# One block of 64-row products per batch in a gated cross-attention and mixture-of-experts kernel: score banks by half of the heads, weighed back into the same banks, and rows of maxima a batch sooner

## The reference, cut to what matters

```python
# per batch t of 32: x[t] is 128 tokens x 128, ctx[t] is 128 keys x 64; 16 heads of 64
x = x + tanh(g_xattn) * xattn(layernorm(x), ctx_512, Wq, Wk, Wv, Wo, bo)
x = x + tanh(g_ffn) * ffn(layernorm(x), ...)      # 32 experts, 8 taken per token, and a shared one

def xattn(q, kv, ...):
    scores = (q @ Wq)_h @ (kv @ Wk)_h.T * scale   # 16 heads, 128 x 128 each
    attn = softmax(scores)
    return concat_h(attn @ (kv @ Wv)_h) @ Wo + bo
```

## Time and profile before

| | |
|---|---|
| median of 3 runs | 651.04 us (650.0 to 651.46) |
| time of the profiled execution | 651.89 us |
| its span, first to last instruction | 650.0 us |
| instructions | 14071 |
| PE busy | 639.0 us (98%) |
| DVE busy | 532.0 us (82%) |
| ACT busy | 389.9 us (60%) |
| POOL busy | 329.3 us (51%) |
| granted clock | full in all 40 slices |

### The profile page before, as it was taken

One profiled execution on the slowest core, in us unless ns is written; L12 is line 12 of the kernel. 1 busy time (PEld: TensorE's weight loads), 2 busy tenths in 40 slices (PEclk: granted clock), 3 DMA queues, 4 the chain that ended last, 5 costly groups with the idle time before them and its releaser, 6 DMA issues.

```text
span 650.0 us, 14071 instructions
## 1 busy us (share of the span) xinstructions
PE 639.0 (98%) x3763; PEld 483.8 (74%) x3763; DVE 532.0 (82%) x1362; ACT 389.9 (60%) x739; POOL 329.3 (51%) x388
## 2 busy tenths in 40 slices
PE   8999999999999999999999999999999999999998
PEld 6657776777766777667558878787887878788786
DVE  6889989888898888988878969778695977869565
ACT  3665666667666676665565555555656555555554
POOL 4336544345534355343404656566575655657563
PEclk9999999999999999999999999999999999999999
DMA  6243343232332324323326555353746535364550
GB/s 181 67 108 80 68 96 85 63 85 60 96 85 60 85 60 96 86 60 82 83 60 172 136 134 131 82 134 85 163 114 134 136 78 132 87 161 114 134 146 17
DMA packets 58429, 65.60 MB, mean 101 GB/s; under 512 B 26256, under 2 KB 35344, under 8 KB 58384
## 3 DMA queue, kind: packets, MB, share of 16 engines
q1 hardware_dynamic: 58384, 65.07, 41.1%
HBM read 61.64 MB, written 2.88 MB: 99 GB/s over the span
## 4 chain that ended last, share of the span: by engine, by line
PE 94%; DVE 2%; ACT 2%; issue 1%; DMA 1%; SPq 0%; DVEq 0%
PE bank L1291 17%; PE bank L1292 17%; PE bank L1293 17%; PE bank L1391 10%; PE bank L1415 9%; PE bank L1338 4%; PE bank L1358 3%; PE bank L1367 2%; PE bank L1361 2%; PE bank L1364 2%; PE bank L1378 2%; DVE halves L880 2%; PE bank L1379 1%; PE bank L1381 1%; ACT halves L628 1%; PE bank L1298 1%
## 5 line engine op out<-in xcount | busy, mean ns | idle before, releaser
L602 POOL TENSOR_TENSOR halves<-area,halves 128x512 fp32r<-128x512 f32 x134 | 174.4, 1302 | 138.5 <-ACT halves L759 133.0
L780 ACT ACTIVATE area<-bank 128x512 f32<-128x512 f32 x136 | 81.4, 599 | 111.1 <-PE bank L1293 108.3
L1247 DVE TENSOR_TENSOR bank<-area,bank 128x512 f32<-128x512 f32 x128 | 88.6, 692 | 50.8 <-PE bank L1293 50.5
L697 ACT ACTIVATE area<-bank 128x512 f32<-128x512 f32 x128 | 69.5, 595 | 100.1 <-PE bank L1367 100.1
L1291 PE MATMUL bank<-x2t_hi,w_hi 128*128 128x512 f32 x272 | 110.3, 405 | 0.1
L1292 PE MATMUL bank<-x2t_hi,w_lo 128*128 128x512 f32 x272 | 107.2, 394 | 0.0
L1293 PE MATMUL bank<-x2t_lo,w_hi 128*128 128x512 f32 x272 | 106.3, 391 | 0.0
L759 ACT ACTIVATE halves<-area 128x512 fp32r<-128x512 f32 x136 | 85.1, 626 | 17.1 <-DVE area L1258 15.9
L889 DVE TENSOR_REDUCE row_max<-bank 128x4 f32<-128x512 f32 x128 | 82.2, 685 | 6.9 <-PE bank L1338 5.9
L1258 DVE TENSOR_TENSOR area<-bank,wbc 128x512 f32<-128x512 f32 x128 | 86.3, 679 | 0.0
L529 POOL TENSOR_TENSOR ctx_hi<-ctx_raw,ones_col 128x128 fp32r<-128x128 f32 x32 | 14.9, 464 | 139.1 <-DMA ctx_raw<-ctx_t 122.1
(11 more groups left out here) (164 smaller groups left out, 1259.4 us busy)
## 6 DMA issues: line engine op xcount, KB each, us to landing
wbc<-rows_dram SPq DMA_DIRECT2D x126, 256.0 KB, 4.5
inverse_bc<-inverse_dram SPq DMA_DIRECT2D x64, 256.0 KB, 3.8
...
ctx_raw<-ctx_t SPq DMA_DIRECT2D x32, 64.0 KB, 3.5
ctx_keys<-ctx_nat SPq DMA_DIRECT2D x32, 64.0 KB, 2.1
...
max_rows<-max_t SPq DMA_DIRECT2D x64, 4.0 KB
```

The costliest lines, as they stand in the source:

```text
L602: nc.gpsimd.tensor_tensor(hid_lo[:, u % SLOTS, :], hid[:, u % HIDS, :], raw(hid_hi[:, u % SLOTS, :]), ALU.subtract).then_inc(hidlo_ready, 1)
L697: nc.scalar.activation(probs_t[:, k, :, :], st_ps[q][:].rearrange("p (h n) -> p h n", h=4), ACT.Exp)\
L780: nc.scalar.activation(silu_g[:, u % 2, :], gate_ps[u % 2][:], ACT.Silu).then_inc(silu_ready, 1)
L1247: nc.vector.tensor_tensor(up_ps[u % UPS][:], silu_g[:, u % 2, :], up_ps[u % UPS][:], ALU.mult)\
```

## The change

The change moves no arithmetic and adds none. It changes four things.

1. The banks: half 0 of the heads has its scores in banks 2 and 3, half 1 in banks 4 and 5. The weighed sums of a half go back into the banks of its scores, once ACT has taken the exponentials. `g_project` borrows banks 0, 1, 6 and 2 inside the attention stage. `scores` of a half now waits until `u_out` of the same half of the batch before has emptied the banks.
2. The order on PE: `max_scores` of half 0, `scores` of both halves and `max_scores` of half 1 follow each other, and all full-row work of the batch stands behind them. `weigh` of half 1 belongs to its own batch and ends it.
3. The row maxima of batch t+2 are transposed, copied out and loaded in batch t, where those of batch t+1 were before.
4. The orders on ACT, DVE and SP follow, and the statistics of x in chunk 0 stand at other places.

```diff
-STATS_AT = {2: (2,), 3: (3, 4), 4: (5,), 5: (6,), 6: (7,)}
+STATS_AT = {1: (2, 3), 2: (4, 5), 3: (6, 7)}
...
-        scores_ps, st_ps, u_ps, ut_ps, small_ps = bank[0:2], bank[2:4], bank[4:6], bank[6], bank[7]
+        scores_ps, ut_ps, small_ps = bank[0:2], bank[6], bank[7]
+        st_ps = (bank[2:4], bank[4:6])
+        u_ps = st_ps
+        g_ps = (bank[0], bank[1], bank[6], bank[2])
...
@@ SP, attention
+                    if not (first and b == 0):
+                        spread_sums(t - 1, (b - 1) % CB)
                     if not last:
                         wait_first(ctx_ready, t + 1)
                         load_raw(b, (t + CB) * P)
-                    if not (last and b == CB - 1):
-                        load_max_row(t + 1, (b + 1) % 2, t - 1)
-                    if not (first and b == 0):
-                        spread_sums(t - 1, (b - 1) % CB)
...
                         store_inverse(t - 1, (b - 1) % 2)
+                    if not (last and b >= 2):
+                        load_max_row(t + 2, b % 2, t)
+                    if not (first and b == 0):
                         spread_inverse(t - 1, (b - 1) % 2)
...
@@ ACT, attention (after exp_of(t, 0, 0) and exp_of(t, 0, 1))
+                    if not first and not last:
+                        probs_high(t)
+                    exp_of(t, 1, 0)
+                    exp_of(t, 1, 1)
+                    if b == 1 and not last:
+                        xt_high(c + 1)
...
+                    for q in range(2):
+                        u_out(t, b, 0, q)
+                    if not (last and b >= 2):
+                        max_out(t + 2, b % 2, 2 * c + b // 2 + 1)
...
                     if b % 2 == 1 and not last:
                         g_high(2 * c + 2 + b // 2, b // 2)
...
+                    for q in range(2):
+                        u_out(t, b, 1, q)
...
@@ DVE, steady_attention
-                    for q in range(2):
-                        take_max(t + 2, b % 2, 0, q)
+                    take_maxima(t + 2, b % 2, 0)
                     batch_stats(t - CB, b)
                     if b == 0:
                         ln_apply(c + 1, t + CB)
+                    batch_mean(t - CB, b)
+                    take_maxima(t + 2, b % 2, 1)
                     probs_low(t)
                     if b == 1:
                         xt_low(c + 1)
-                    for q in range(2):
-                        take_max(t + 2, b % 2, 1, q)
                     residual(t - 3)
-                    batch_mean(t - CB, b)
                     if b == CB - 1:
                         keep_means(t - b - CB)
+                    if b % 2 == 0:
+                        invert(t - 1, (b - 1) % 2)
+                    normalise(t - 2, (b - 2) % CB, 0)
                     if b % 2 == 1:
                         g_low(2 * c + 2 + b // 2, b // 2)
                         invert(t - 1, (b - 1) % 2)
-                    normalise(t - 2, (b - 2) % CB, 0)
-                    if b % 2 == 0:
-                        invert(t - 1, (b - 1) % 2)
                     normalise(t - 2, (b - 2) % CB, 1)
...
@@ PE, scores
-                wait(pe, exp_ready, 4 * t + 2 * h)
+                wait(pe, u_ready, 4 * t + 2 * h - 2)
...
@@ PE, attention (all batches but the first)
+                        if not (last and b >= 2):
+                            max_scores(t + 2, b + 2, nth + 1, 0)
+                        scores(t, b, nth, 0, nth + 1, projections)
+                        scores(t, b, nth, 1, nth + 1, None)
+                        if not (last and b >= 2):
+                            max_scores(t + 2, b + 2, nth + 1, 1)
+                    if b == 1:
                         transpose_norm(c + 1, ut_ps)
...
                     if not (first and b < 3):
                         project_out(t - 3, (b + 1) % 2, t + 1 if last and b == CB - 1 else t + 2)
...
+                    for q in range(2):
+                        if first or last:
+                            weigh(t, b, 0, q, c + 1)
+                        else:
+                            weigh_halves(t, b, q)
+                    if not (last and b >= 2):
+                        transpose_max(t + 2, b % 2)
...
                     if b % 2 == 1 and not last:
-                        g_project(b // 2, c + 1, ((max_ready, 4 * (t + 2) + 3), (exp_ready, 4 * t + 3)))
...
+                        g_project(b // 2, c + 1, ((max_ready, 4 * (t + 2) + 3), (u_ready, 4 * t)), range(4), g_ps)
+                    for q in range(2):
+                        weigh(t, b, 1, q, c + 1)
```

233 lines of the change are left out of this document (94 added, 139 removed).

## The result

The changed kernel takes 662.38 us (median of 4 runs), the kernel before 651.19 beside it: ratio 1.0168, 95% interval 1.0144 to 1.0192. The forecast of 646.2 with a range to 651.3 was wrong, and on the wrong side. The profiled execution has a span of 660.5 us against 650.0, so 10.5 us have to be found.

The account below looks back on a forecast made before the run. PE was taken as the bound, busy 639.0 of 650.0 us, with DVE second to watch. Gains of 15.6 us less losses of 10.8 gave -4.8 from a median of 651.04, so 646.2 us, range 641.5 to 651.3.

Parts of the forecast that it names:

- On SP `load_max_row` now stands ahead of `spread_inverse` ... the inverses are wanted a batch later, so I cost it at nothing: SP's queue: the new order delays the inverses by two issues, which was costed at nothing.
- The price that I named in case the cover were gone: DVE at normalise: it would stand 1.3 us if the inverses were not wanted a batch later.
- DVE enters the loop late: 0.7 ... and 0.8: Entry to the steady loop: waits of 0.7 us at DVE's first maxima and 0.8 at its first probs_low.
- The last chunk, 2.5 us: Last chunk's first batch: PE waits 2.5 us at transpose_max, because residual stands late in DVE's list.
- waits of 0.5 + 1.1 + 0.25 + 0.8: Chunk 0: waits for first-batch maxima, before g_project and at transpose_norm in the second, and for fourth-batch maxima, in us.
- A pair of mode changes with the slower first products behind them: PE, steady batches: two fewer array-mode switches (0.19) and faster first products (0.05 and 0.06) gain 0.30 us each.
- The 0 that I took for the scores of one half behind those of the other: PE: scores of one half directly behind the other's, in other banks, cost 0 extra; bounds 0 and 0.05 us.
- The 0.34 behind `g_project`: PE behind an odd batch: the 0.34 us wait for g_low goes, counted 13 times for 4.4 us.
- The wait for the maxima in even batches: Second max_scores in both even batches of a chunk: PE waits 0.2 us, eleven times, 2.2 us in all.
- that for `probs_low` in the first batch of a chunk: Third product of weigh_halves: PE waits 0.4 us in each steady chunk but the first, 2.0 us in all.
- POOL did not meet `probs_low`: Rival: POOL's work overlaps probs_low on DVE in each steady batch and slows it, about 656 us; chance 0.12.
- The waits that ate the gain: Rival: 0.2 us more waiting in each of 24 batches makes 4.8, so about 651 us; chance 0.13.

Follow-up runs that it names:

- experiment 1: Changed kernel with the four guess levels of rstd moved ahead of normalise and g_low in chunk 0's last batch on DVE; span 653.8 us, ratio to before 1.0086.
- experiment 3: Changed kernel with DVE's invert in even steady batches back between the two halves of normalise; span 652.2 us, ratio to before 1.0047.
- experiment 9: Changed kernel with 20 unused transposes added on PE ahead of transpose_max in the last chunk's first batch; span 659.0 us, ratio to before 1.0138.
- experiment 12: Changed kernel with the guess levels early and invert back between the halves of normalise; median 647.85 us, span 645.1, ratio to before 0.9939.
- experiment 8: The kernel before, with DVE's invert ahead of both halves of normalise in even steady batches; span 653.8 us, ratio to before 1.0035.
- experiment 4: Changed kernel with spread_sums issued ahead of spread_inverse on SP, at the batch's end; span 658.7 us, ratio to before 1.0136.
- experiment 10: Experiment 7's kernel with probs_low and xt_low ahead of the second maxima on DVE; span 667.4 us, ratio to before 1.0269.
- experiment 5: Changed kernel with guess levels early, residual first in the last chunk's first batch, and invert between the halves of normalise; span 645.6 us, ratio to before 0.9937.
- experiment 11: Experiment 5's kernel with DVE's order of xt_low and statistics in chunk 0 edited to fill the wait before invert; span 645.3 us, ratio to before 0.9910.
- experiment 6: Changed kernel with ln_apply, xt_low and g_low moved earlier on DVE in chunk 0's batch 1; median 667.27 us, ratio to before 1.0250.
- experiment 7: Experiment 3's kernel with the 64-row block split, the second max_scores behind project_out in the steady loop; span 705.0 us, ratio to before 1.0920.

## Why the prediction was wrong, step by step

The measured median is 16.2 us above the forecast. By the runs 4.8 of it are batch 4 (experiment 1), 8.4 the place of `invert` (experiment 3) and 1.7 the clock in batch 28 (12.73, against 11.06 to 11.12 in experiments 1, 9 and 12, where it stayed full): 14.9 together. The other 1.3 us are a balance of smaller misses, of which chunk 0 (+2.3) and the last batches (-1.5) are the largest. Without the first two the median is 1.7 from the forecast (experiment 12).

- **The failing step is the sentence "On SP `load_max_row` now stands ahead of `spread_inverse` ... the inverses are wanted a batch later, so I cost it at nothing".** I followed `inverse_bc` and not what stands behind it in the same queue, `spread_sums`, nor its consumer: the change had moved `invert` ahead of `normalise` in even batches, and no step of the prediction prices that move. Each half of it alone costs little: with `invert` ahead in the kernel before, batches 8 to 27 are the same, though the first steady chunk loses 2.3 (experiment 8); with the new SP order and the old DVE order, the steady chunks are as short as forecast (experiment 3). Experiment 8 also has PE's slack of before, so it doesn't say what SP's order alone is worth. The price that I named in case the cover were gone, 1.3 us at DVE, is the right size (0.8 to 1.9), at the neighbouring instruction. Undoing DVE's half of the pair gave back 7.1 us in batches 8 to 27 (experiment 3), turning the order on SP 3.4 (experiment 4).
- **"DVE enters the loop late: 0.7 ... and 0.8"** counts DVE's own list. The four guess levels are small there, 0.7 us in all, but they start twelve steps on POOL that `ln_apply` waits for, with POOL's split of the keys behind them. Moved from before `g_low` to after it, they cost 4.8 us. With them early, batch 4 is 9.21 against 8.56, so +0.65 where 1.5 less the gains was said.
- **The last chunk, 2.5 us:** 2.29, right. The half clock behind it was not in the sum: 1.67.
- **Chunk 0:** it grew by 2.8. By the forecast's terms it should have grown by about 0.5 (waits of 0.5 + 1.1 + 0.25 + 0.8, less 3 x 0.24 for mode changes and the 1.4 for `max_rows`), or 0.2 with the 0.34 behind its first `g_project`. PE's excesses after are 0.4 in the first batch, 0.99 before `g_project` and 1.0 in the fourth batch, near what was said; `transpose_norm` has 1.06 where 0.25 was said, and 0.55 + 0.70 behind `g_low` was not in the list. There `invert` waits 2.42 for the sums of batch 0, the same pair again. The terms were small ones; their sum was 2.3 short or more. That the last batches gained more than was counted made up for half of it, by luck.
- **The gains are there.** A pair of mode changes with the slower first products behind them, 0.30 said; splitting the block costs 0.27 (experiment 10). One part of the 0.30 did not come: the first product of `weigh_halves` takes 0.31 to the next in steady batches after, against 0.29 before and the cadence of 0.23, so the 0.06 for each of 24 batches, 1.4 us, were not gained. The 0 that I took for the scores of one half behind those of the other is right (0.23). The 0.34 behind `g_project` is gone: L1339 to L1359 is 0.11 in every steady batch after. A steady chunk without most of the wait for `sums` is 0.98 to 1.07 us shorter than before (experiments 3, 5, 11 and 12); 1.1 was said. The wait for the maxima in even batches is 0.1 (0.2 said), that for `probs_low` in the first batch of a chunk 0.26 (0.4 said); these smaller waits hide the missing 0.06. The last batches gained 3.1 (batches 29 to the end), more than the 1.6 counted there (0.9 and 3 x 0.24).
- **The rivals.** POOL did not meet `probs_low`: L898 has 0.68 in steady batches after, and the one at 0.89 stands in batch 4. The waits that ate the gain, 0.13, come nearest, but 0.2 in each batch is not what happened: two single places of 4 to 5 us, and one wait of up to 1.2 in every second batch. I had this sort of wait in mind only as a sum of small margins.

What stays open: why the clock fell behind the wait of 2.29 in batch 28 of the changed kernel and of experiment 10, partly in experiment 3, and not in experiments 1, 4, 6, 7 and 12, with the same wait. No run here tells that apart.
